# An adaLN-style block with attention and adapters: one x row tile's split, the rounding of the row maxima and the last steps' fillers are placed anew

## The chip, the cores and the metric

The kernel runs on one core of a Trainium2 chip. The metric is the device time in microseconds of one execution. A core has a matrix engine (TensorE, PE), three others (VectorE, DVE; ScalarE, ACT; GpSimd, POOL), a queue for transfers (SyncE, SP) and 16 DMA engines. Each engine works off its own instructions in the order in which they are written, and waits for the others through counting semaphores.

## The reference, cut to what matters

```python
def reference(x, ...):            # x: (8, 256, 1024) float32
    # 1. linear layer with a LoRA adapter per batch row, chosen by itok_B_0_23
    c = x @ W.T + b + 2.0 * (x @ A[itok]) @ Bm[itok]
    # 2. attention: 32 query heads, 8 key/value heads of 32, softmax over 256 keys
    q, k, v = c @ w_q, c @ w_k, c @ w_v
    weights = softmax(q @ k.T / sqrt(32));  x = x + (weights @ v) @ w_o
    # 3. per-row weight matrix (itok_B_3_7), then a routed low-rank FFN, top 2 of 4 experts
    z = x @ weight[itok2].T
    x = x + sum over experts of gate_e(z) * (z @ A_e.T) @ B_e.T * 4
```

## The kernel before

Matrices in float32 are split in a rounded high part (fp32r) and a low part, value minus high part, and multiplied as high x high + high x low + low x high. A split is thus two instructions: ScalarE rounds, and VectorE (for some tiles GpSimd) subtracts.

There are three stages. `fold_stage` multiplies W into the projection weights. `attend_stage` runs four pairs of batch rows (`PAIRS`), and in each pair 16 steps (`STEPS`), 64 steps in all; a step n is one key/value head of one batch row. `finish_stage` multiplies by w_o, adds to x, and does the routed FFN; its first pieces are woven into the last steps of attention through the functions `ahead_*`, and its `first()` and `second()` follow.

In a step TensorE's order is written out in `tensor.step`: scores 0 and 1 of head n (L926); the first part of the projection work that the table `WORK` gives this step (units such as q6, q7 for this pair and v0, v1 for the next; L854, L876 to L880); the outputs of head n-3 (L950) and their sums of exponentials (L954, from GpSimd's `p_sum`); the transpose of the maxima of head n-1 (L961); transposed scores 0 and 1 of head n-2 (L937); scores 2 and 3 of head n; the second part of the work; transposed scores 2 and 3. Projection units take turns in two PSUM banks (`bank`), and a unit starts when the one two before it has been read out (`free`).

VectorE's order in a step (`vector.step`): maxima 0 and 1 (L770), splits of x named in `X_LO[(s, 0)]` (L493), low parts of the units that the step before finished (`late(n - 1)`, L739), then maxima 2 and 3, then `split_maxima(n)`: a cast of the 128x8 negated maxima to fp32r (L776) and the subtraction for their low parts (L778), then `X_LO[(s, 1)]` and the reductions of value units (`soon(n, 1)`). In step 0 the low part of q1 is taken between maxima 1 and 2. Scores i of a head wait for maxima i-2 (`s_max`), the transpose waits for the low parts of the maxima (`nmax_lo`).

ScalarE's order (`scalar.step`): the copy of the transposed maxima (L699), exponentials 0 and 1 (L681), the output copy (L689), value copies (L667), `X_HI[(s, 0)]` (L489), exponentials 2 and 3, high parts of q and k units (`late(n)`, L646, four instructions of which the second signals a half), `X_HI[(s, 1)]`. GpSimd adds the exponentials (L630, `p_sum`) two steps after their scores, and takes the lower part of x tiles 2 and 4 (`X_LO_POOL`). SP queues the loads of x and of Wo, and the copies inside the chip.

```python
X_HI = {(10, 1): range(4), (11, 0): [4], (12, 0): [5, 6], (12, 1): [7]}
X_LO = {(11, 0): [0, 1], (11, 1): [3], (12, 1): [5, 6], (13, 0): [7]}
X_LO_POOL = {10: 2, 11: 4}
```

In the last steps (s = 12 and up of pair 3, and steps 64 to 66) `ahead_tensor` fills TensorE with w_o tiles (`one_tile`, L1239; tile 7 is done in two halves) and with rows of the first batch row's cond2 matrix (`cond_row`, L1284). A cond row is loaded by GpSimd (`load_cond`, L1187, into one of four buffers, after a register load of its index at L1183), rounded by ScalarE (L1265), and its low part is taken by VectorE (L1269). `residual` (L1230) adds a w_o tile to x; a tile waits for the residual two before it. `middle` (L1580) multiplies x by the turned product `g_t`. `first()` and `second()` are written out for each engine.

## Time and profile before

| | us |
|---|---|
| median of 3 runs | 1009.52 |
| lowest, highest | 1008.81, 1012.29 |
| the profiled execution | 1010.05 |
| its span | 1008.4 |
| TensorE busy | 987.5 (98%) |
| VectorE busy | 625.9 (62%) |
| ScalarE busy | 453.6 (45%) |
| GpSimd busy | 247.2 (25%) |

The span is the time from the first to the last instruction that the profiler recorded; 1.65 us of the execution lie around it. The granted TensorE clock was 0.998 over the span. A view of waits puts the idle time of an engine just before an instruction down to the one that released it. A line in the timeline gives start, length, engine, line, operation, what it writes and reads, the number of merged instructions, and in brackets the idle time before it with its releaser. Steps 0 to 63 run from 187.6 to about 692 us; pair changes (steps 9 to 14) lie at 250 to 298, 379 to 428 and 509 to 557 us and look alike; the first is shown.

### The profile page before, as it was taken

What the parts mean: (1) busy time and instruction counts of PE and PEld (TensorE: products, weight loads), DVE (VectorE), ACT (ScalarE), POOL (GpSimd) and SP (SyncE); (2) the same over time, 40 slices, a digit from 0 to 9 for tenths busy, and PEclk for the clock granted to TensorE, in tenths of its full rate; (3) what the DMA queues carried; (4) which work ended last, traced back from release to release, by engine and by line L of the source; (5) the groups of instructions that cost most, each with busy time, mean ns of one, the idle gap of its engine ahead of it and who ended that gap; (6) DMA issues with size and microseconds to landing.
All of it is one profiled execution on the core that took longest, in us unless ns stands there. A gap on an engine that the chain in (4) does not pass through costs nothing.

```text
span 1008.4 us, 16074 instructions
## 1 busy us (share of the span) xinstructions
PE 987.5 (98%) x6228; PEld 769.9 (76%) x6228; DVE 625.9 (62%) x1028; ACT 453.6 (45%) x806; POOL 247.2 (25%) x234
## 2 busy tenths in 40 slices
PE   9999999999999999999999999999999999999996
PEld 6878788777687776877777777786787778778775
DVE  6671822686946778467786688766664654654443
ACT  6121322365744657456665566747441432332221
POOL 1000001033422434223343247645110110110001
PEclk9999999999999999999999999999999999999999
DMA  7030411111411124111142424264999579463432
GB/s 274 0 105 1 136 48 56 43 44 39 128 36 44 50 59 123 44 44 49 44 114 79 110 74 138 86 170 185 276 298 251 165 248 243 143 223 108 164 125 84
DMA packets 72395, 117.33 MB, mean 116 GB/s; under 512 B 7698, under 2 KB 55186, under 8 KB 70816
## 3 DMA queue, kind: packets, MB, share of 16 engines
q1 hardware_dynamic: 62592, 81.70, 28.5%
q0 software_dynamic: 9728, 34.61, 10.0%
q8 instruction: 50, 0.82, 0.4%
q14 instruction: 25, 0.20, 0.1%
HBM read 86.38 MB, written 18.89 MB: 104 GB/s over the span
## 4 chain that ended last, share of the span: by engine, by line
PE 92%; DVE 4%; ACT 1%; POOL 1%; issue 1%; DMA 1%; POOLq 0%; ACTq 0%
PE psP L854 21%; PE psW L1239 17%; PE psF L292 12%; PE psG L1284 8%; PE psO L950 6%; PE psS L926 6%; PE psT L937 5%; PE psX L1580 3%; PE psO L954 3%; DVE nmax L770 2%; PE psF L303 2%; PE psP L876 2%; DVE q_stack L739 1%; PE psP L878 1%; PE psM L961 1%; PE psP L880 1%
## 5 line engine op out<-in xcount | busy, mean ns | idle before, releaser
L630 POOL TENSOR_TENSOR p_sum<-probs 128x512 f32<-128x512 f32 x128 | 168.5, 1317 | 331.7 <-ACT probs L681 331.7
L854 PE MATMUL psP<-x_hl,wq 128*128 128x512 f32 x960 | 237.2, 391 | 0.2 <-DVE v_sb L760 0.2
L770 DVE TENSOR_REDUCE nmax<-psS 128x2 f32<-128x512 f32 x256 | 164.5, 684 | 96.2 <-PE psS L926 91.8
L854 PEld LDWEIGHTS psP<-x_hl,wq 128*128 128x128 f32 x960 | 173.4, 188 | 31.2 <-DVE v_sb L760 0.4
L681 ACT ACTIVATE probs<-psT 128x512 f32<-128x512 f32 x256 | 139.0, 595 | 74.2 <-PE psT L937 73.4
L1239 PE MATMUL psW<-o_split,wq 128*128 128x512 f32 (+1 forms) x600 | 137.5, 383 | 0.0
L1239 PEld LDWEIGHTS psW<-o_split,wq 128*128 128x128 f32 x600 | 108.8, 188 | 21.4
L1269 DVE TENSOR_TENSOR cond_lo<-cond_raw,cond_hi 128x1024 fp32r<-128x1024 f32 x64 | 78.3, 1240 | 54.8 <-ACT cond_hi L1265 54.3
L1265 ACT ACTIVATE cond_hi<-cond_raw 128x1024 fp32r<-128x1024 f32 x64 | 66.5, 1057 | 82.9 <-PE psG L1284 70.2
L739 DVE TENSOR_TENSOR q_stack<-psP,q_stack 32x512 fp32r<-32x512 f32 x128 | 87.8, 686 | 10.2 <-ACT q_stack L646 8.3
L926 PEld LDWEIGHTS psS<-k_stack,q_stack 96*128 96x128 f32 x512 | 79.0, 189 | 16.5 <-DVE q_stack L739 2.1
L1187 POOL DMA_DIRECT2D cond_raw<-in_cond x64 | 33.9, 530 | 232.8 <-PE psG L1284 232.8
L937 PE MATMUL psT<-q_stack,k_stack 98*128 98x512 f32 x256 | 86.8, 418 | 0.0
L926 PE MATMUL psS<-k_stack,q_stack 96*128 96x256 f32 x512 | 84.6, 285 | 1.9 <-DVE nmax L770 1.3
L646 ACT ACTIVATE q_stack<-psP 32x512 fp32r<-32x512 f32 x128 | 75.1, 587 | 17.3 <-PE psP L861 15.8
L292 PE MATMUL psF<-q_hi,w_hi 128*128 128x512 f32 x184 | 71.8, 390 | 0.0
L292 PE MATMUL psF<-q_lo,w_hi 128*128 128x512 f32 x184 | 71.6, 389 | 0.0
L292 PE MATMUL psF<-q_hi,w_lo 128*128 128x512 f32 x184 | 71.6, 389 | 0.0
L950 PE MATMUL psO<-probs,v_sb 128*32 128x256 f32 x1024 | 68.5, 385 | 0.0
L699 ACT ACTIVATE nmax_rows<-psM 16x128 f32<-16x128 f32 x64 | 17.0, 266 | 105.1 <-PE psM L961 104.7
L950 PEld LDWEIGHTS psO<-probs,v_sb 128*32 128x32 f32 x1024 | 26.7, 109 | 30.1 <-issue 16.3
L1239 PE MATMUL psW<-wq 128*128 128x256 f32 x384 | 49.4, 283 | 0.0
(155 smaller groups left out, 1378.4 us busy)
## 6 DMA issues: line engine op xcount, KB each, us to landing
cond_raw<-in_cond POOLq DMA_DIRECT2D x64, 512.0 KB, 4.8
x_raw<-in_xT SPq DMA_DIRECT2D x32, 256.0 KB, 3.2
o_scratch<-o_sb SPq DMA_DIRECT2D x64, 128.0 KB
q_stack<-q_stack SPq DMA_DIRECT2D x31, 256.0 KB, 2.9
q_raw<-in_Wqkv SPq DMA_DIRECT2D x24, 256.0 KB, 3.9
o_pair<-rden_scratch SPq DMA_DIRECT2D x24, 256.0 KB, 9.0
o_pair<-o_scratch SPq DMA_DIRECT2D x6, 1024.0 KB, 13.9
w_raw<-in_W SPq DMA_DIRECT2D x8, 512.0 KB, 7.8
```

The source lines that it names most:

```text
L292: mm = pe.matmul(psF[:, bank(j, m)], w[:, k, m * P:(m + 1) * P], q[:, k], start=(k == 0 and i == 0), stop=(k == KT - 1 and i == 2))
L630: pool.tensor_tensor(p_sum[:, heads], probs[:, 0, heads], probs[:, 1, heads], ALU.add).then_inc(sum_done, 1)
L681: nc.scalar.activation(probs[:, i % 2, (i // 2) * 512:(i // 2 + 1) * 512], psT[:, i % 2], ACT.Exp, scale=ATT_SCALE).then_inc(exp_done, 1)
L739: ins = dve.tensor_tensor(to(h), both(psP[32 * h:32 * h + 32, bank(p, u)]), f(hi(h)), ALU.subtract)
L770: dve.tensor_reduce(nmax[:, n % 2, 2 * hp:2 * hp + 2, qt], psS[:, i % 2].rearrange("p (h k) -> p h k", h=2), AX.X, ALU.max, negate=True).t ...
L854: mm = pe.matmul(out, wq[:, i, w, k * P:(k + 1) * P], x[:, k, part], start=(k == 0 and n_ == 0), stop=False)
L926: mm = pe.matmul(psS[:, i % 2, j * T:(j + 1) * T], q_stack[0:96, slot, c, 2 * hp + j, qt * P:(qt + 1) * P], k_stack[0:96, c, g], start=Tru ...
L937: pe.matmul(psT[:, kt], k_stack[0:98, c, g, kt * P:(kt + 1) * P], q_stack[0:98, slot, c, 2 * hp:2 * hp + 2].rearrange("p h t -> p (h t)"), ...
L950: pe.matmul(psO[HD * h:HD * h + HD, 0], v_sb[p % 2][:, c, kt, g], probs[:, kt, h * T:(h + 1) * T], start=(kt == 0), stop=(kt == KK - 1))
L1239: mm = pe.matmul(out, wq[:, k, w, m * P:(m + 1) * P], o(part, k), start=(k == 0 and j == 0), stop=(k == KT - 1 and j == 2))
L1269: dve.tensor_tensor(cond_lo[r % RAW][:], cond_raw[r % RAW][:], f(cond_hi[:, r % SPLIT]), ALU.subtract).then_inc(cond_lo_done, 1)
L1284: mm = pe.matmul(psG[0:EC, half], a[:, k], w[:, half * 512:(half + 1) * 512], start=(k == 0 and i == 0), stop=(k == KT - 1 and i == 2))
```

## The change

The fourth row tile of x (tile 3) has its lower part taken in part 0 of step 11 and not in part 1; the rounding of tile 4 moves from part 0 to part 1. The maxima are rounded by ScalarE (a Copy activation, 128x8, SBUF to SBUF) behind exponentials 2 and 3 of the step, and VectorE takes their low parts one step on, behind maxima 0 and 1. In step 0 the low part of q1 moves behind maxima 3. In the last steps the first half of w_o tile 7 goes to step 64 ahead of cond row 0, its second half to step 65, and the halves that stood in `first()` and `second()` each move up by one place; their residuals move with them. The load of cond row 6 is issued by GpSimd between the two `p_sum` of the last head, and not behind them. ScalarE copies the turned product before it rounds cond row 9.

```diff
@@ -339,8 +339,8 @@
 
 
 X_LOAD = {(9, 0): [0, 1], (9, 1): [2], (10, 0): [3, 4], (10, 1): [5], (11, 0): [6, 7]}
-X_HI = {(10, 1): range(4), (11, 0): [4], (12, 0): [5, 6], (12, 1): [7]}
-X_LO = {(11, 0): [0, 1], (11, 1): [3], (12, 1): [5, 6], (13, 0): [7]}
+X_HI = {(10, 1): range(4), (11, 1): [4], (12, 0): [5, 6], (12, 1): [7]}
+X_LO = {(11, 0): [0, 1, 3], (12, 1): [5, 6], (13, 0): [7]}
 X_LO_POOL = {10: 2, 11: 4}
 SEQ = ["v0", "v1", "v2", "v3", "t", "k0", "q0", "q1", "q2", "r0", "r1", "q3", "k1", "q4", "q5", "q6", "q7"]
 NS = len(SEQ)
@@ -626,6 +626,8 @@
                 pool.wait_ge(exp_done, TILES * n + 2 * hp + 2)
                 if n and hp == 0:
                     pool.wait_ge(pv_done, n)
+                if n == N - 1 and hp == 1:
+                    ahead.gpsimd_last(pool)
                 heads = slice(hp * T2, (hp + 1) * T2)
                 pool.tensor_tensor(p_sum[:, heads], probs[:, 0, heads], probs[:, 1, heads], ALU.add).then_inc(sum_done, 1)
             if p + 1 < PAIRS and s + 2 in X_LO_POOL:
@@ -680,6 +682,11 @@
                 act.wait_ge(pv_done, n)
             nc.scalar.activation(probs[:, i % 2, (i // 2) * 512:(i // 2 + 1) * 512], psT[:, i % 2],
                                  ACT.Exp, scale=ATT_SCALE).then_inc(exp_done, 1)
+
+        def round_maxima(n):
+            act.wait_ge(s_max, TILES * (n + 1))
+            nc.scalar.activation(nmax_parts[:, n % 2, 0:8], nmax[:, n % 2].rearrange("p h q -> p (h q)"),
+                                 ACT.Copy).then_inc(nmax_hi, 1)
 
         def copy_o(n):
 
@@ -713,6 +720,8 @@
             if 2 <= n <= N + 1:
                 exp(n - 2, 2)
                 exp(n - 2, 3)
+            if n < N:
+                round_maxima(n)
             if more and s == 8:
                 split_a_hi(act, p + 1)
             for unit_ in late(n):
@@ -772,8 +781,6 @@
 
         def split_maxima(n):
             flat = nmax[:, n % 2].rearrange("p h q -> p (h q)")
-            dve.wait_ge(s_max, TILES * (n + 1))
-            dve.tensor_copy(nmax_parts[:, n % 2, 0:8], flat).then_inc(nmax_hi, 1)
             dve.wait_ge(nmax_hi, n + 1)
             dve.tensor_tensor(nmax_parts[:, n % 2, 8:16], flat, f(nmax_parts[:, n % 2, 0:8]),
                               ALU.subtract).then_inc(nmax_lo, 1)
@@ -784,10 +791,12 @@
             if n < N:
                 maxima(n, 0)
                 maxima(n, 1)
+            if 1 <= n <= N:
+                split_maxima(n - 1)
             if more:
                 for k in X_LO.get((s, 0), ()):
                     split_x_lo(dve, p + 1, k, x_lo_done)
-            for unit_ in late(n - 1) if n else [(0, "q1")]:
+            for unit_ in late(n - 1):
                 evacuate(*unit_)
             for unit_ in soon(n, 0):
                 if unit_[1] != "q0":
@@ -796,7 +805,8 @@
             if n < N:
                 maxima(n, 2)
                 maxima(n, 3)
-                split_maxima(n)
+            if n == 0:
+                evacuate(0, "q1")
             if p and n < N and s == 6:
                 invert(dve, p - 1)
             if more and s == 8:
@@ -1189,7 +1199,7 @@
 
     def gpsimd(pool):
         for n in range(B):
-            load_cond(pool, n, range(6, KT) if n == 0 else range(KT))
+            load_cond(pool, n, range(7, KT) if n == 0 else range(KT))
 
         pool.wait_ge(gated_done, B)
         for j in range(YT):
@@ -1315,6 +1325,8 @@
             dve.tensor_tensor(ra_lo[:], ra_raw[:], f(ra_hi[:]), ALU.subtract).then_inc(ra_lo_done, 1)
         if part == 1 and s == 14:
             normalise(dve, 1)
+        if part == 1 and s == 17:
+            residual(dve, KT - 1)
         for r in ROWS_LO.get((s, part), ()):
             cond_row_lo(dve, r)
         if part == 0 and s == 16:
@@ -1331,12 +1343,15 @@
         if s in ROWS_LOAD:
             load_cond(pool, 0, ROWS_LOAD[s])
 
+    def ahead_gpsimd_last(pool):
+        load_cond(pool, 0, [6])
+
     def ahead_tensor(pe, n, part):
         m = FIRST_TILES.get((n - LAST, part))
         if m is not None:
             one_tile(pe, 0, m)
-        if (n - LAST, part) == (17, 0):
-            one_tile(pe, 0, KT - 1, range(4))
+        if (n - LAST, part) in ((16, 0), (17, 0)):
+            one_tile(pe, 0, KT - 1, range(4) if n - LAST == 16 else range(4, KT))
         if (n - LAST, part) == (18, 1):
             pe.wait_ge(o_lo_done, 2)
             one_tile(pe, 1, 0, range(4))
@@ -1375,8 +1390,8 @@
             nc.scalar.activation(fb_stack[:], fb_raw[:], ACT.Copy).then_inc(fb_hi_done, 1)
             copy_g(0)
             cond_row_hi(act, KT)
+            turn_copies(0)
             cond_row_hi(act, KT + 1)
-            turn_copies(0)
 
         def second():
             gates(0)
@@ -1498,8 +1513,8 @@
         def first():
             cond_row_lo(dve, 6)
             dve.memset(beats[:], 0.0).then_inc(chain, 1)
+            residual(dve, KT)
             cond_row_lo(dve, 7)
-            residual(dve, KT - 1)
             before.invert(dve, PAIRS - 1)
             dve.wait_ge(fb_hi_done, 1)
             dve.tensor_tensor(fb_stack[ER:P], fb_raw[ER:P], f(fb_stack[ER:P]), ALU.subtract).then_inc(fb_lo_done, 1)
@@ -1507,10 +1522,10 @@
             cond_row_lo(dve, KT + 1)
 
         def second():
-            residual(dve, KT)
+            residual(dve, KT + 1)
             gates(0)
             for m in range(KT):
-                if m:
+                if m > 1:
                     residual(dve, KT + m)
                 if m < 6:
                     cond_row_lo(dve, KT + m + 2)
@@ -1613,18 +1628,19 @@
         def first():
 
             cond_row(pe, 5)
-            one_tile(pe, 0, KT - 1, range(4, KT))
+            one_tile(pe, 1, 0, range(4, KT))
             cond_row(pe, 6)
             cond_row(pe, 7)
-            one_tile(pe, 1, 0, range(4, KT))
+            one_tile(pe, 1, 1, range(4))
             turn_g(0)
-            one_tile(pe, 1, 1, range(4))
+            one_tile(pe, 1, 1, range(4, KT))
             middle(0)
 
         def second():
             cond_row(pe, KT)
             for m in range(1, KT - 1):
-                one_tile(pe, 1, m, range(4, KT) if m == 1 else range(KT))
+                if m > 1:
+                    one_tile(pe, 1, m)
                 cond_row(pe, KT + m)
             cond_row(pe, KT + 7)
             one_tile(pe, 1, KT - 1, range(4))
@@ -1681,7 +1697,7 @@
             y_two(B - 1, j, last_bank(j), y_done)
 
     ahead.sync, ahead.gpsimd, ahead.scalar, ahead.vector = ahead_sync, ahead_gpsimd, ahead_scalar, ahead_vector
-    ahead.tensor = ahead_tensor
+    ahead.tensor, ahead.gpsimd_last = ahead_tensor, ahead_gpsimd_last
     st.sync, st.gpsimd, st.scalar, st.vector, st.tensor = sync, gpsimd, scalar, vector, tensor
     return st
```

## Rows read from the trace of the kernel before

**Rows 1.** The profile's page: busy time of each engine, and the chain.

```profile
PE 987.5 (98%) x6228; PEld 769.9 (76%) x6228; DVE 625.9 (62%) x1028; ACT 453.6 (45%) x806; POOL 247.2 (25%) x234
...
PE 92%; DVE 4%; ACT 1%; POOL 1%; issue 1%; DMA 1%; POOLq 0%; ACTq 0%
```

**Rows 2.** Waits of TensorE: released by whom; us in total, times, longest.

```profile
PE psP L876 <- DVE q_stack L739: 2.6, 3, 0.9
PE psP L876 <- DVE x_hl L493: 1.8, 3, 0.6
...
PE psS L926 <- DVE nmax L770: 1.3, 2, 0.8
```

**Rows 3.** Timeline of TensorE, steps 12 to 14 of the first pair.

```profile
268.96 0.28 PE L880 MATMUL psP<-v_lo,x_hl 128*128 128x256 f32 x1
...
269.84 0.40 PE L876 MATMUL psP<-v_hi,x_hl 128*128 128x288 f32 x1 [0.60 <-DVE x_hl L493]
...
273.95 0.37 PE L876 MATMUL psP<-v_hi,x_hl 128*128 128x288 f32 x1 [0.86 <-DVE q_stack L739]
...
283.31 0.40 PE L876 MATMUL psP<-v_hi,x_hl 128*128 128x288 f32 x1
```

**Rows 4.** Groups by line: busy us, mean ns, idle before.

```profile
L776 DVE CAST nmax_parts<-nmax 128x8 fp32r<-128x8 f32 x64 | 38.8, 607 | 2.2
...
L778 DVE TENSOR_TENSOR nmax_parts<-nmax,nmax_parts 128x8 fp32r<-128x8 f32 x64 | 16.0, 250 | 2.2
...
L1354 ACT ACTIVATE gate<-shift 128x8 f32<-128x8 f32 x8 | 1.7, 208 | 26.6 <-DVE shift L1461 26.6
...
L511 ACT ACTIVATE v_hi<-a_raw 128x128 fp32r<-128x128 f32 x8 | 2.0, 308 | 0.0
```

**Rows 5.** Timeline of VectorE, steps 9 to 12, and step 15.

```profile
256.19 0.68 DVE L776 CAST nmax_parts<-nmax 128x8 fp32r<-128x8 f32 x1
...
256.99 1.28 DVE L770 TENSOR_REDUCE nmax<-psS 128x2 f32<-128x512 f32 x2
258.31 2.79 DVE L739 TENSOR_TENSOR q_stack<-psP,q_stack 32x512 fp32r<-32x512 f32 x4
261.12 1.29 DVE L770 TENSOR_REDUCE nmax<-psS 128x2 f32<-128x512 f32 x2
...
271.01 2.79 DVE L739 TENSOR_TENSOR q_stack<-psP,q_stack 32x512 fp32r<-32x512 f32 x4
...
308.82 1.22 DVE L778 TENSOR_TENSOR nmax_parts<-nmax,nmax_parts 128x8 fp32r<-128x8 f32 x1
```

**Rows 6.** Timeline of GpSimd, steps 10 and 15.

```profile
257.20 1.28 POOL L630 TENSOR_TENSOR p_sum<-probs 128x512 f32<-128x512 f32 x1 [0.36 <-ACT probs L681]
...
308.74 1.28 POOL L630 TENSOR_TENSOR p_sum<-probs 128x512 f32<-128x512 f32 x1 [7.71 <-ACT probs L681]
```

**Rows 7.** Timeline of ScalarE, end of step 9.

```profile
257.01 2.39 ACT L646 ACTIVATE q_stack<-psP 32x512 fp32r<-32x512 f32 x4
```

**Rows 8.** Timeline of TensorE, step 1.

```profile
192.99 1.01 PE L926 MATMUL psS<-k_stack,q_stack 96*128 96x256 f32 x4 [0.85 <-DVE nmax L770]
...
196.36 0.27 PE L961 MATMUL psM<-id_sb,nmax_parts 128*16 128x128 f32 x1
```

**Rows 9.** GpSimd: a register load, the DMA behind it, the last p_sum.

```profile
L608 POOLq TENSOR_LOAD <-idx_a x1: 283/283/283, 205.8 to 205.8; - x1
...
206.97 0.53 POOL L609 DMA_DIRECT2D a_raw<-in_lora_A  x1 [0.51 <-issue]
...
704.74 1.29 POOL L630 TENSOR_TENSOR p_sum<-probs 128x512 f32<-128x512 f32 x1 [0.57 <-ACT probs L681]
705.96 1.09 POOL L1187 DMA_DIRECT2D cond_raw<-in_cond  x2
```

**Rows 10.** Timeline of TensorE, step 64 and `first()`.

```profile
692.45 0.65 PE L1284 MATMUL psG<-cond_hi,ra_hi 128*68 128x512 f32 x2 [0.26 <-DVE nmax L770]
...
715.52 0.68 PE L1284 MATMUL psG<-cond_hi,ra_hi 128*68 128x512 f32 x2 [0.51 <-DVE cond_lo L1269]
```

**Rows 11.** Busy time by window: 713 to 750 us; clock, DMA share and GB/s last.

```profile
713.00:750.00 37.00, 35.93 (x251) 30.71 (x252) 24.44 (x40) 15.78 (x16) 4.23 (x8) 1.00 1.06 316
```

## Prediction

> **What bounds the kernel now.** I read the busy shares and the chain first: TensorE is busy 98% of the span and holds 92% of the chain that ended last, VectorE 4% [rows 1]. A gain has to come out of TensorE's gaps, so its waits are the next view: the three largest, on q low parts, on x's low parts and on maxima, sum to 5.7 us [rows 2]. These are idle times behind a modelled end; from start to start a gap is longer: the last product of one x tile starts at 268.96, the first of the next usually 0.12 us on, here at 269.84, so 0.76 us is lost where the view says 0.60 [rows 3]. Counted that way over TensorE's timeline, the gaps that the change can reach are: in steps 0 to 3 before maxima 1.2 and 0.9; in each of three pair changes 0.45 (maxima), 0.76 (x's fourth row tile), 1.03 (the bank of q7) and 0.30 (value copies); and between 692 and 721 0.54, 0.37, 0.89, 0.68 and 0.41. That is 2.1 + 7.6 + 2.9 = 12.6 us. The question is which of them only change their name.
>
> **VectorE's relief.** The cast goes: 64 of 607 ns, 38.8 us of VectorE; the subtraction stays (250 ns mean) [rows 4]. But a cast such as that of 256.19 ends at 256.87, 0.03 after the p_sum that ran beside it on GpSimd: most of its time is a wait. The moved subtraction stands after the next step's first two maxima. In step 10 these started at 256.99; with the cast and the subtraction gone from before them they can start at 256.51 (0.44 after their scores) and end at 257.79, in the middle of the p_sum of 257.20 to 258.48 [rows 5, 6]. Does a subtraction wait for it too? Its usual row is 0.17 us; but at 308.82, begun 0.08 after a p_sum, it took 1.22 and ended with it [rows 5, 6]. I take "it waits": it ends at 258.50 and the q evacuation starts at 258.54, where it was 258.31.
>
> The Trainium skill (SBUF — State Buffer, "SBUF: two separate sides") has the rule behind this: a VectorE instruction with two SBUF inputs and a GpSimd one that reads SBUF exclude each other for the whole instruction; the row at 308.82 agrees. By the 0.17 us of the usual row the subtraction would end at 257.99, by the rule at 258.50.
>
> Even without that hold little is won, for ScalarE arrives at the same time: its new rounding stands before its q copies. I price it at 0.2 us by the 128x8 exponential, 208 ns; bounds 0.15 (part of it overlaps its neighbour) and 0.31 (the copies of 128x128) [rows 4]. Copies that began at 257.01 begin at 257.2 and are half done at 258.4 instead of 258.2 [rows 7]. So evacuations that open the second half of a step move back by 0.2 to 0.3 us.
>
> **Where that costs.** The maxima of 261.12 become 261.35 [rows 5], and TensorE, which already waits for them at 261.96, goes on 0.24 later; that is inside the pair sum below. Elsewhere: 0.1 each in step 3 of pairs 1 and 2, 0.2 in step 3 of pair 3, 0.25 in step 11 of pair 3, where scores stand within 0.2 us of their maxima: +0.65. The other steps have over 0.8 us between maxima and scores; no cost there.
>
> **The split of x, three times.** The fourth tile's lower part moves ahead of the second-half maxima and ends near 267.3; TensorE's 0.76 goes [rows 3], so the products behind it come 0.57 earlier, the 0.24 counted. ScalarE, relieved of the fifth tile's rounding here, begins its last two exponentials at 268.44; their p_sum runs from 269.6 to 270.89; the subtraction is held until 270.92, and the evacuation of q7 starts at 270.95 instead of 271.01 [rows 5]. Its end frees the bank that TensorE waits for at 273.95 [rows 3]. So the 0.76 is given back to that wait but for 0.06. The fifth tile (rounded from 272.0 to 272.6, lower part on GpSimd until 273.9) is wanted at 276.4: hidden, with 2.5 us to spare; what queues behind its rounding on ScalarE, a row copy and two exponentials, comes 0.4 later under as much cover. Two steps on, the value block's reductions no longer stand behind cast and subtraction, 0.8 us, ScalarE's copy comes as much earlier, and the 0.30 before 283.31 goes [rows 3]. Per pair -0.36, in all -1.1.
>
> **Steps 0 to 3.** q1's evacuation now follows the second maxima. The scores of 192.99 lose their wait, 1.2 us with the pair behind them [rows 8]. But the evacuation (2.79 from 191.88) ends at 194.67, the maxima of step 1 at 195.98, the subtraction at 196.18, and the transpose, which TensorE now reaches at 195.1, cannot start before 196.3: it stood at 196.36 [rows 8]. ScalarE's rounding waits in step 1 for maxima that end at 198.2 and holds q2's copies behind it, 1.6 us; q2 is read in step 4, so that is hidden. Step 3 starts at 204.07 instead of 204.21: -0.14.
>
> **The last steps (from 692).** Half of tile 7 now stands before the first cond row: 12 products, 1.43 us. It fills the 0.54 before 692.45 [rows 10] and 0.27 of the 0.37 before 700.61, and from there on one more half tile is done by each point. Against that, GpSimd's load of cond row 6 now stands between the wait for the last exponentials and the last p_sum, with SP's queue untouched. Exposed are a register load and the issue: such a pair takes from 205.8 to 206.97 until the DMA starts and 0.53 for itself, 1.7 us; the lower bound is the 0.51 of idle printed there plus 0.53, 1.04. The p_sum of 704.74 is that much later, and the last sums (at 706.08, with under 0.1 us of slack) move to about 708.4 with the shift of the half tile [rows 9]. The load itself, issued at 705.96 before, is issued at about 706.5: not earlier. Row 7's load behind it moves from 706.51 to 708.4 and lands near 713.1 to 714; TensorE wants the row at 716.3 and it is ready at 716.8, after rounding, a residual and 1.23 of subtraction. Sum: gone 0.54 + 0.27 + 0.89 + 0.68 + 0.41 = -2.8 (the last three are the waits for cond rows, such as that before 715.52, and for the g copies [rows 10]); new 1.7 and 0.5. SP starts its big loads when the last output is copied, 2.3 us later, into a stretch in which the DMA engines are full (share 1.06 [rows 11]); one of them landed 0.6 us before VectorE used it, and the residual behind is waited for: 0.3 to 0.8, I take 0.4. Together -0.2; bounds -1.3 and +2.0.
>
> **Sum.** +0.65 - 1.1 - 0.14 - 0.2 = -0.8 us. Against the profiled execution's 1010.05 (1008.4 of span and 1.65 around it) that is 1009.25; the median of the runs is 0.53 below it, so 1008.7.
>
> **Rivals.**
> (a) The gaps close for good: 2.1 in steps 0 to 3, 3 x 1.06 for tile and value copies, 2.9 at the end, nothing given back: -8.2, 1001.3. For it: 38.8 us off the engine that ends most of TensorE's waits [rows 2, 4]. Against: two independent releases (the held subtraction, ScalarE's half) stand at the same 258.5, and the transpose of step 1 hangs on the moved subtraction. Half of it, -4 (1005.5), is the least that I would call faster; it takes an undelayed p_sum (-1.7) and a q7 evacuation that starts right behind its maxima (3 x 0.5).
> (b) Slower by one mechanism: the register load before the last p_sum shifts the chain of the last output and with it the o and x loads on full DMA engines. If TensorE waits for them in the second stage (725 to 750) by the full 2.3 us instead of 0.4, the whole is +1.1; if their landing stretches twice as far, +4, 1013.5. It decides once the residual before tile 14 is over 3 us late.
> (c) ScalarE's rounding waits for late maxima and blocks its queue: q copies, then exponentials. At 0.2 us in half of 64 steps, +6, 1015. Against it: before most of its row copies ScalarE is idle for 1 us or more.
> (d) The waits move and little else happens: my forecast.
>
> **Chances and range.** Within 0.3% (3.0 us, about what a measurement tells from no change), which is (d) with the mild ends of (a) and (b): 0.67. (a) from its half on 0.21; (b) and (c) beyond 3 us 0.12. So faster 0.21, same 0.67, slower 0.12. The likeliest case alone has 1007.0 to 1011.3: the last steps' bounds, and the rounding at 0.15 or 0.31 in ten places. With the cases of both signs, 1005.0 to 1011.6.
>
> **What the profile after would show.** Right: subtractions of 0.6 to 0.7 us where p_sum runs beside them; TensorE's wait for the tile gone, the one for q7 still about 1 us; the one for value copies gone; the last p_sum over 1 us after the last exponential, a register load between. Wrong: subtractions of 0.17 in all steps; a q7 wait under 0.5; cond row 6 landing before 710; the chain running through DMA between 735 and 750; or exponentials that follow the rounding late in most steps.

## Result and profile after

The change made the kernel slower: 1015.64 us median (1009.80 to 1018.40, 17 runs) against 1009.51 (1008.21 to 1012.41, 17 runs), ratio 1.0047 with a 95% interval of 1.0035 to 1.0059. Forecast was 1008.7, within 1005.0 to 1011.6. The profiled execution took 1016.2 us with a span of 1014.5, 6.1 more than before. The runs of the changed kernel scatter: 4 of 17 lie under 1011, the others between 1012.0 and 1018.4. The trace is of one of the latter; none exists of the four.

The page of the changed kernel, busy shares and chain, where [rows 1] stand for before. SP's queue is new in the chain, and DMA has 3% where it had 1%:

```profile
PE 987.4 (97%) x6228; PEld 769.9 (76%) x6228; DVE 609.8 (60%) x964; ACT 461.5 (45%) x870; POOL 246.0 (24%) x234
...
PE 89%; DVE 5%; DMA 3%; SPq 1%; issue 1%; POOL 1%; ACT 1%; POOLq 0%; ACTq 0%
```

TensorE's waits after (by whom it was released; total, times, longest). Against [rows 2] the wait for x's low parts is gone, the one for q's grew, and two are new: the residual (`x_even`, L1240, L1230 before) and the last p_sum:

```profile
PE psW L1249 <- DVE x_even L1240: 6.0, 2, 5.0
PE psP L886 <- DVE q_stack L748: 3.4, 3, 1.1
PE psO L964 <- POOL p_sum L632: 2.0, 1, 2.0
```

**The attention steps** gained as meant. TensorE's timeline after, which answers to [rows 3]: the x tile's products follow each other 0.12 us apart, and the wait for q7's bank is longer (1.31 us from start to start, 1.03 before):

```profile
268.22 0.28 PE L890 MATMUL psP<-v_lo,x_hl 128*128 128x256 f32 x1
268.34 0.29 PE L886 MATMUL psP<-v_hi,x_hl 128*128 128x288 f32 x1
...
272.87 0.37 PE L886 MATMUL psP<-v_hi,x_hl 128*128 128x288 f32 x1 [1.14 <-DVE q_stack L748]
```

Measured from step 0 (187.58 before, 187.09 after: that half microsecond arose in the fold, ahead of every edited line, and is noise: step 0 starts between 186.7 and 187.6 in all seventeen traces) step 4 starts 0.51 earlier, step 16 1.01, step 62 1.49. These distances repeat well: from step 0 to step 62 the five traces with the attention of before take 488.26 to 488.38 us, the ten with that of after 486.72 to 486.85.

**From step 62 to the end** 8.1 us were lost: 332.6 us before, 340.6 after. All of it lies ahead of `middle(1)`, the second product of x with a turned g: from its start to the end all traces of all kernels take 253.4 us. GpSimd and TensorE around the last p_sum, after ([rows 9] before):

```profile
704.94 0.55 POOL L1197 DMA_DIRECT2D cond_raw<-in_cond  x1 [2.11 <-issue]
705.52 1.27 POOL L632 TENSOR_TENSOR p_sum<-probs 128x512 f32<-128x512 f32 x1
```
```profile
706.84 0.64 PE L964 MATMUL psO<-p_sum,ones 128*32 128x256 f32 x8 [2.03 <-POOL p_sum L632]
```

That is 2.2 us. Still, `middle(0)` starts 0.8 us earlier than before, with half a tile more done. From step 62 to that point TensorE takes 46.1 us where it took 44.9, of which 1.43 are the additional products: so far nothing is lost. From `middle(0)` to `middle(1)` it takes 41.2 us instead of 34.3. SP stores the last outputs 0.8 us later than before (708.17, before 707.41), but begins load_o(2) 1.2 us earlier (712.64, before 713.84). SP's queue, then VectorE, then TensorE, in the second stage:

```profile
719.31 4.02 SPq L475 DMA_DIRECT2D rden_scratch<-rden_sb  x1
723.37 3.44 SPq L1119 DMA_DIRECT2D o_pair<-rden_scratch  x4
726.86 0.85 SPq L1121 DMA_DIRECT2D o_pair<-o_scratch  x1
```
```profile
747.46 2.29 DVE L1212 TENSOR_TENSOR o_pair<-o_pair 128x2048 f32<-128x2048 f32 x1 [5.80 <-DMA o_pair<-o_scratch]
749.66 0.42 DVE L1240 TENSOR_TENSOR x_even<-x_even,psW 128x256 f32<-128x256 f32 x1
```
```profile
740.58 3.12 PE L1249 MATMUL psW<-wq 128*128 128x256 f32 x24 [0.95 <-DVE x_even L1240]
...
750.14 4.62 PE L1249 MATMUL psW<-wq 128*128 128x256 f32 x24 [5.04 <-DVE x_even L1240]
```

Read it backwards: TensorE waits for a residual; the residual stands in VectorE's queue behind the normalisation of o(3); that one waits for load_o(3)'s last transfer, issued at 726.86 and landed 20.6 us later (before: issued 724.27, landed 741.0, used at 741.59). And 24 products behind the wait take 4.62 us where the same 24 took 3.12 ten microseconds earlier. The windows 740 to 760, before and then after (busy us of TensorE, its weight loads, VectorE, ScalarE and GpSimd; granted clock, DMA share and GB/s last), show why: the granted clock was at the upper of its two levels (2.4 GHz) before, and 0.91 of that in the mean after, behind a pause of 5 us.

```profile
740.00:760.00 20.00, 19.82 (x143) 17.31 (x142) 15.46 (x24) 9.42 (x10) 2.12 (x4) 1.00 0.86 265
```
```profile
740.00:760.00 20.00, 14.38 (x92) 12.45 (x93) 11.62 (x11) 8.26 (x7) 2.11 (x4) 0.91 0.70 233
```

### The profile page after: what moved, and what is told of

Read it like the earlier page. It is cut to its first block, busy times and chain, and to the rows that moved or that the text cites. A ratio compares the mean times of both kernels' runs of the same rounds, so it can differ in the third digit from the quotient of the medians.

```text
span 1014.5 us, 16077 instructions
## 1 busy us (share of the span) xinstructions
PE 987.4 (97%) x6228; PEld 769.9 (76%) x6228; DVE 609.8 (60%) x964; ACT 461.5 (45%) x870; POOL 246.0 (24%) x234
## 3 DMA queue, kind: packets, MB, share of 16 engines
q0 software_dynamic: 9728, 34.61, 10.5%
## 4 chain that ended last, share of the span: by engine, by line
PE 89%; DVE 5%; DMA 3%; SPq 1%; issue 1%; POOL 1%; ACT 1%; POOLq 0%; ACTq 0%
PE psP L864 20%; PE psW L1249 16%; PE psF L292 12%; PE psG L1294 7%; PE psS L936 6%; PE psO L960 6%; PE psT L947 6%; PE psO L964 3%; PE psX L1595 2%; DVE q_stack L748 2%; DMA o_pair<-o_scratch 2%; PE psP L886 2%; PE psF L303 2%; PE psP L888 2%; DVE nmax L779 1%; PE psP L890 1%
## 5 line engine op out<-in xcount | busy, mean ns | idle before, releaser
L936 PEld LDWEIGHTS psS<-k_stack,q_stack 96*128 96x128 f32 x512 | 79.2, 189 | 15.9 <-issue 2.4
L1249 PEld LDWEIGHTS psW<-wq 128*128 128x128 f32 x384 | 49.3, 196 | 8.3 <-DVE x_even L1240 6.9
```

The lines of the kernel that those rows point to most:

```text
L936: mm = pe.matmul(psS[:, i % 2, j * T:(j + 1) * T], q_stack[0:96, slot, c, 2 * hp + j, qt * P:(qt + 1) * P], k_stack[0:96, c, g], start=Tru ...
L1249: mm = pe.matmul(out, wq[:, k, w, m * P:(m + 1) * P], o(part, k), start=(k == 0 and j == 0), stop=(k == KT - 1 and j == 2))
```

## Experiments

All ratios are to the kernel before on the same chip, with 95% intervals; a ratio can differ a little from the quotient of the two medians, since the runs scatter unevenly. Where two variants were measured on different chips, their ratios say more than their medians.

### The change in parts

Theory T says: row 6's load delays the last p_sum, with it SP's loads, and o(3) lands late. Its rivals put the loss on the 2 us by which everything comes earlier (A) or on the new order of tiles, rows and residuals (F).

**e1_no_row6** is the change without this part:

```diff
-                if n == N - 1 and hp == 1:
-                    ahead.gpsimd_last(pool)
...
-            load_cond(pool, n, range(7, KT) if n == 0 else range(KT))
+            load_cond(pool, n, range(6, KT) if n == 0 else range(KT))
```

> The whole change, but cond row 6 is loaded after the last p_sum, as before. Theory T (the load before the last p_sum delays the p_sum, the last output copy and with it SP's big loads; load_o(3) then lands 6 us late and TensorE waits 5 us for the residual in front of tile 14): the o loads land as before, the wait of 5 us is gone, and the attention part's gain stays: 1006 to 1008, ratio 0.996 to 0.999. Rival A (the attention part's shift by 2 us is what collides with the DMA traffic) and rival F (the order of row loads, residuals and tiles at the end does it): the wait of 5 us stays, 1012 to 1015. Rival R: row 6 lands too late for its new place, a new wait of 1 to 2 us before cond row 6, 1008 to 1010.

**e2_row6_only** is the converse: the kernel before with only that load moved.

> The kernel before with cond row 6's load moved ahead of the last p_sum and nothing else. Theory T: p_sum 1.7 to 2.2 us later, the last output copy as much, the loads behind it land 3 us or more later and the normalisation of o(3) holds the residual behind it: +4 to +7 us, 1014 to 1017, ratio 1.004 to 1.007. Rivals A and F: only the p_sum wait itself, less what later waits give back, +1 to +2 us, ratio 1.001 to 1.002.

**e3_attn_only** has the x split, the rounding on ScalarE and the new place of q1's evacuation (the copy out of PSUM with its low part), and the last steps of before; **e4_tail_only** the last steps' part and the attention of before.

> The x split, the maxima's rounding on ScalarE and q1's evacuation moved; the last steps are those of before. By my sum of the prediction -0.6 us; by the step starts of the changed kernel's trace -1.8 to -2.0 us: 1007.5 to 1009, ratio 0.998 to 0.9995. Rival A: everything 2 us earlier is what makes the big loads collide: a wait of some us for a residual between 740 and 752, 1011 to 1014.

> The last steps' part alone: half tiles, row and residual order, row 6's load ahead of the last p_sum; the attention steps are those of before. Theory T or rival F: the wait of 5 us in front of tile 14 is there, 1014 to 1018, ratio 1.004 to 1.008 (the changed kernel without the gain of 1.5 to 2 us in the attention part). Rival A: no such wait, 1009 to 1011.

Measured: e1 1008.91 us, ratio 0.9992 (0.9981 to 1.0003); e2 1018.22, 1.0082 (1.0068 to 1.0095); e3 1008.55, 0.9986 (0.9970 to 1.0002); e4 1015.63, 1.0063 (1.0043 to 1.0083). Rival A falls with e3, rival F with e1: the one load of 512 KB, placed one instruction further ahead, costs 6.7 us with the rest of the change and 8.8 without it (by the ratios 5.5 and 8.3). Rival R has no large part: e1 waits 0.25 us for one row's low part. But e1 isn't as fast as T had it, and e2 is slower. TensorE in e1, second stage, has two waits where before had none:

```profile
737.31 3.13 PE L1247 MATMUL psW<-wq 128*128 128x256 f32 x24 [0.46 <-DVE x_even L1238]
...
742.76 3.14 PE L1247 MATMUL psW<-wq 128*128 128x256 f32 x24 [0.92 <-DVE x_even L1238]
```

From start to start they are 0.62 and 1.09 us. From step 62 to `middle(0)` the fillers save e1 2.3 us (43.99 us with 1.43 of additional products, before 44.87), and between there and `middle(1)` 1.8 come back (34.61 us with 1.43 less to do, before 34.27): TensorE meets the o loads that much earlier. What is left over is too little for single traces: to the end e1 takes 332.0 us, e3 332.3 and the kernel before 332.5, but two more kernels with the same last steps as before 331.5 (e8 below) and 333.5 (e7 below). By the ratios e1 is no faster than e3.

e2 lost its time elsewhere. ScalarE, then TensorE, in e2:

```profile
723.30 1.06 ACT L1267 ACTIVATE cond_hi<-cond_raw 128x1024 fp32r<-128x1024 f32 x1 [3.01 <-DMA cond_raw<-in_cond]
724.26 0.67 ACT L1372 ACTIVATE g_t<-psX 128x272 f32<-128x272 f32 x2
```
```profile
708.09 2.80 PE L1241 MATMUL psW<-wq 128*128 128x256 f32 x12
...
724.98 6.79 PE L1585 MATMUL psX<-g_t,x_even 128*128 128x68 f32 x32 [3.29 <-ACT g_t L1372]
731.52 1.10 PE L1286 MATMUL psG<-cond_hi,ra_hi 128*68 128x512 f32 x2
...
736.20 0.63 PE L1286 MATMUL psG<-cond_hi,ra_hi 128*68 128x512 f32 x2
```

ScalarE's copies of g stood behind the rounding of row 9, whose load was late. TensorE paused 3.3 us, and then two products of 128x512 took 1.10 us instead of 0.63: it ran at the lower level, 1.2 GHz, until about 735 (0.50 in the windows 728 to 731 and 731 to 734). `middle(0)` took 6.79 us; in e1 the same 32 products take 3.69. Behind the pause of 2.1 us for the p_sum, too, the clock fell here (0.57 from 708 to 710, 0.58 to 712): 12 products took 2.80 us, where 1.60 is usual. So e2's loss in its trace is two pauses, 5.5 us from start to start, and the clock behind each, 1.2 and 3.1 us in these two groups alone, less some waits of before that are gone. The change's order (copies of g ahead of row 9's rounding) takes just this trap away, and steps into the next.

### The p_sum's delay, or the load's place?

**e13_reg_only** delays the last p_sum in the kernel before by one register load and moves no DMA:

```diff
+                if n == N - 1 and hp == 1:
+                    pool.value_load(idx_sb[0:1, 0:1], min_val=0, max_val=7)
```

> The kernel before, with one more register load ahead of the last p_sum, whose value nothing uses, and no DMA moved. Theory T: the p_sum is 0.5 to 1.2 us late, the last output copy and SP's loads as much: +1 to +4 us, 1010.5 to 1013.5; that prices the register load alone. Rival D (only the moved DMA matters): within 0.5 us of the kernel before. Rival C (a TensorE pause of this length costs more by its clock): a stretch below 0.95 of the clock between 705 and 760.

**e10_row6_early** puts row 6's load one p_sum further ahead, at `hp == 0`, before the wait for the exponentials.

> The whole change, but row 6's load stands one p_sum further ahead, before the wait for the exponentials of the last step's first half, where GpSimd idles 1.3 us. Theory T (what costs is the delay of the last p_sum by register load and issue, with all that hangs on it): the wait of 2.2 us before the last sums goes, load_o(3) lands before 742: 1006.5 to 1009, ratio 0.997 to 0.9995. Rival D (the earlier row load itself crowds the DMA engines and delays SP's loads): no wait before the sums, but load_o(3) still lands after 745, 1012 to 1015.

**e19_rows67_ahead** puts the loads of rows 6 and 7 both there, `load_cond(pool, 0, [6, 7])` at `hp == 1`.

> The whole change, but the loads of rows 6 and 7 both stand ahead of the last p_sum, back to back as they were before. Rival D2 (splitting the two loads is what slows the engines between 709 and 724): rates there back to 320 and 290 GB/s, load_o(3) lands by 743, 1010 to 1012 in spite of a p_sum 0.6 us later still. Theory Q: the p_sum and load_o(3) come out later still, 1015.5 to 1019.

e13: 1010.49, 1.0012 (0.9993 to 1.0032). The register load made the p_sum 0.56 us later (idle 1.13 instead of 0.57 before it), TensorE waited 0.67 for it, and nothing else moved: load_o(3) landed at 740.8. T's first half is right, and at this size cheap. e10: 1015.43, 1.0039 (1.0018 to 1.0059), though TensorE's pause for the p_sum fell from 2.2 to 1.1 us: load_o(3) landed at 747.0, though SP had begun load_o(2) at 710.3, 3.5 us earlier than before (1.2 counted from step 62). So T falls: neither the delay of the p_sum nor a late start of SP's loads is what costs. e19: 1011.38, 1.0018 (1.0004 to 1.0033), with the longest wait for the p_sum of all (2.42 us from start to start). VectorE and TensorE in e19:

```profile
742.77 2.29 DVE L1213 TENSOR_TENSOR o_pair<-o_pair 128x2048 f32<-128x2048 f32 x1 [2.08 <-DMA o_pair<-o_scratch]
```
```profile
707.05 0.64 PE L964 MATMUL psO<-p_sum,ones 128*32 128x256 f32 x8 [2.24 <-POOL p_sum L632]
...
745.45 3.14 PE L1250 MATMUL psW<-wq 128*128 128x256 f32 x24 [1.31 <-DVE x_even L1241]
```

With both loads ahead the change is 3 to 4 us faster than with row 6's alone (2.9 by the ratios, 4.3 by the medians), although the p_sum comes later still. The profiled execution of e19 is its fastest of ten. Why it helps isn't shown: D2 had asked for 320 and 290 GB/s between 709 and 724, and there were 253. And in e2, where the two loads are also apart, load_o(3) landed early (738.0): being apart isn't enough to delay it.

### What o(3) waits for on its way

Theory O: with row 6 ahead, load_o(2) gets onto the engines before row 9's load and both suffer. **e14_o2_behind_row9** holds load_o(2) back in the changed kernel, **e16_row9_late** holds row 9's load back in the kernel before, by three register loads.

```diff
         before.load_den(sp, PAIRS - 1)
+        sp.wait_ge(cond_used, 7)
         load_o(sp, 2)
```

> The whole change, but SP waits, between the load of the denominators and load_o(2), until cond row 6 has been used, 2.3 us behind the issue of row 9's load. Theory O (the runs with row 6's load ahead are slow where load_o(2) gets onto the DMA engines before row 9's load does, because the earlier row 6 lets the denominators return sooner; then row 9 lands 9 instead of 6 us after its issue, o(2) after 18 instead of 13 us, and load_o(3) near 747): load_o(2) begins 2.4 us later and still lands earlier, near 729 to 731; row 9 lands near 719; load_o(3) lands by 743; the wait of 5.2 us before tile 14 is under 2 us: 1009 to 1011.5, ratio 1.000 to 1.002. Rival T (what counts is how late SP's loads start): load_o(2) later by 2.4 us makes it worse, 1016 to 1020. Rival D2 (the order of rows 6 and 7 alone slows the engines): no difference from the changed kernel, 1015 to 1016.

> The kernel before, with row 9's load alone held back by three register loads on GpSimd, some 1.5 to 2 us, so that it comes amid load_o(2)'s first transfers; TensorE's own use of row 9 has 5 us to spare. Theory O: row 9 takes 8 us or more to land, load_o(2) lands after 732, load_o(3) after 744, TensorE waits 2 to 5 us for a residual between 740 and 752: 1012 to 1016, ratio 1.003 to 1.006. Rivals T and D2 (row 9's place does not matter by itself): within 0.7 us of the kernel before.

e14: 1016.29, 1.0065 (1.0044 to 1.0086). Row 9 landed at 718.0 (after: 721.7), as O had it, but load_o(2) at 731.7 and load_o(3) at 747.2: O falls for the changed kernel. e16: 1016.58, 1.0055 (1.0033 to 1.0077), but not by O's way: row 9 landed at 722.3, and the trap of e2 closed (a pause of 4.5 us before `middle(0)`, and half speed from 723 until 732). O asked for a late load_o(3); it landed at 741.0.

Theory Q: SP issues load_o(3) too late, behind row 12's load. **e17_o3_first** is the changed kernel with load_o(3) ahead of the store of the last reciprocals, which it doesn't need.

```diff
-        before.store_rden(sp, PAIRS - 1)
         load_o(sp, 3)
+        before.store_rden(sp, PAIRS - 1)
```

> The whole change, but SP loads o(3) before it waits for the last reciprocals and stores them, not after (o(3) needs only reciprocals stored long before). Theory Q (with row 6's load ahead, load_o(3) gets out of SP's queue behind the load of row 12 instead of 2 us ahead of it, as in every kernel with the 5 us wait; then rows 12 to 14 share the engines with it): the o(3) loads are issued 1 to 4 us earlier, ahead of row 12's, and land by 743; the wait before tile 14 is under 2 us: 1009 to 1011.5, ratio 1.000 to 1.002. Rival K (SP issues only as the engines free its earlier loads, whatever the order): o(3)'s last load is still issued at 726 and lands at 746 to 748, 1014 to 1016.

e17: 1013.72, 1.0030 (1.0011 to 1.0048), with runs at 1010 and at 1016. In the profiled one SP began load_o(3) at 715.6 instead of 723.4, and still issued its last transfer at the same time as before:

```profile
715.59 11.28 SPq L1119 DMA_DIRECT2D o_pair<-rden_scratch  x4
726.90 1.42 SPq L1121 DMA_DIRECT2D o_pair<-o_scratch  x1
```

So rival K is right for this stretch: an SP instruction that is reached earlier just stands longer. The table sets the kernels side by side, all from traces, one of each: GB/s from 709 to 724, when load_o(2)'s fourth transfer of reciprocals landed, when SP issued load_o(3)'s last transfer, when GpSimd issued row 12's load, when load_o(3) landed, and TensorE's wait before tile 14 (start to start). The execution traced isn't always typical of its kernel: for instance those of e1, e4 and e19 took 1.3 to 1.9 us less than the median, that of e17 3.1 more.

| kernel | GB/s | o(2) fourth | o(3) issued | row 12 issued | o(3) landed | wait |
|---|---|---|---|---|---|---|
| before | 301 | 724.5 | 724.3 | 726.5 | 741.0 | 0 |
| e1 | 308 | 722.3 | 721.9 | 723.4 | 740.1 | 1.1 |
| e3 | 299 | 722.6 | 722.4 | 724.1 | 739.3 | 0 |
| e7 | 255 | 725.7 | 725.1 | 725.3 | 741.0 | 0 |
| e8 | 305 | 722.7 | 723.4 | 725.4 | 740.3 | 0 |
| e9 | 307 | 722.2 | 723.4 | 723.9 | 740.6 | 0 |
| e13 | 304 | 724.4 | 724.1 | 725.9 | 740.8 | 0 |
| e18 | 314 | 720.8 | 721.9 | 723.6 | 740.2 | 0 |
| e19 | 253 | 723.0 | 724.3 | 725.9 | 742.7 | 1.5 |
| e2 | 263 | 723.4 | 724.7 | 735.0 | 738.0 | 0 |
| e16 | 279 | 725.6 | 726.8 | 733.9 | 741.0 | 0 |
| e4 | 249 | 727.7 | 727.0 | 727.1 | 745.0 | 2.7 |
| after | 266 | 727.5 | 726.9 | 725.7 | 747.4 | 5.2 |
| e5 | 254 | 727.0 | 726.1 | 725.5 | 747.6 | 0 |
| e10 | 241 | 726.7 | 726.4 | 724.6 | 747.0 | 6.7 |
| e14 | 256 | 726.9 | 726.0 | 725.2 | 747.2 | 6.5 |
| e17 | 246 | 727.8 | 726.9 | 726.5 | 747.3 | 4.9 |

In every trace load_o(3)'s last transfer goes out within 1.3 us of the landing of load_o(2)'s fourth one. Where it lands at 745 or later, these two stand at 726 to 728, otherwise at 721 to 726, but for e16's issue at 726.8. The rate between 709 and 724 doesn't tell: e7 and e19 have 255 and 253 GB/s and an early landing. How long the transfer takes goes with row 12's load: 20.4 to 21.6 us in the five kernels in which that went out first, 15.9 to 18.4 in the ten in which it went out up to 2.3 us behind, and 13.3 and 14.2 in e2 and e16, where a pause of TensorE had held it back to 735.0 and 733.9. So a later issue is paid for twice, once by itself and once because GpSimd's row loads are then on the engines first; no run moved the row loads alone to prove it. The Trainium skill (DMA: Bandwidth & Descriptors, "Queues, rings and completion order") says that an engine takes turns between its queues packet by packet; the longer landing beside GpSimd's row loads agrees with it. Why load_o(2) is 3 us later with row 6's load ahead, and not when row 7's goes with it (e19) nor in e2, no run here settles.

### The cover on VectorE

Cover is here the work that TensorE can still do before something late holds it up.

**e5_norm_late** is the whole change with o(3) normalised two tiles later; **e9_no_row6_norm_late** is e1 with the same edit; **e18_e9_o3_first** adds e17's edit to e9.

```diff
-                if m in (2, 3):
-                    normalise(dve, m)
+                if m in (2, 5):
+                    normalise(dve, 2 if m == 2 else 3)
```

> The whole change, but VectorE normalises o(3) two tiles later (behind the residual and the lower part of m = 5), so that a late load_o(3) holds no residual in front of tiles 12 to 14. If the wait of 5.2 us in front of tile 14 is the landing of load_o(3) held in VectorE's queue: the wait and the stretch at 0.91 of the clock behind it go, 1008 to 1010.5, ratio 0.999 to 1.001, while load_o(3) still lands near 747. Rival L (the loads of x, not o(3), hold the residuals, or TensorE meets the next late load as soon as it gets there): another wait of 2 us or more between 740 and 760, 1012 to 1015.

> Row 6 loaded after the last p_sum, as before, and o(3) normalised two tiles later; the rest of the change stands. The waits of 0.62 and 1.09 us for residuals at 737 and 743 that the kernel without the row load has: the second goes, the first (behind o(2)'s normalisation) stays: 1 us less than that kernel, 1007.5 to 1008.5, ratio 0.998 to 0.999. Rival: DMA landings set this stretch whatever VectorE's order, no difference from the kernel without the row load, 1008.9.

> The best kernel so far (row 6 behind the last p_sum, o(3) normalised two tiles later) with load_o(3) ahead of the store of the reciprocals. Theory Q: o(3) lands 1 to 3 us earlier, but nothing waits for it there any more; the wait of 0.6 us before middle(1) or the residual's stays: within 0.5 us of that kernel, 1006.5 to 1007.5, ratio 0.996 to 0.998. Rival K: the reciprocals' store and x_odd's loads are later, a new wait further on: 1008 or more.

e5: 1011.23, 1.0015 (1.0002 to 1.0027), a little more than expected and 4.4 us less than the change by the medians and 3.2 by the ratios. load_o(3) lands as late as before the edit, but no residual that TensorE soon needs stands behind its normalisation any more. VectorE and TensorE in e5:

```profile
747.64 2.29 DVE L1212 TENSOR_TENSOR o_pair<-o_pair 128x2048 f32<-128x2048 f32 x1 [1.10 <-DMA o_pair<-o_scratch]
```
```profile
752.84 0.71 PE L1584 MATMUL psY<-id_sb,g_sb 68*128 68x68 f32 x8 [1.63 <-ACT g_sb L1377]
```

The 5 us became 1.8 (start to start) at the next customer, g's copy, which stands behind the rounding of o(3) in ScalarE's queue. e9: **1007.00 us (1006.66 to 1007.57, 9 runs), ratio 0.9966 (0.9954 to 0.9978)**, faster than both kernels and with the least scatter of all. Of e1's two waits the second is gone, as expected; 0.45 us of idle time before g's turn are new. The 2.6 us that the ratios put between e1 and e9 don't show in the traces, which take 1007.34 and 1007.57: the one of e1 is its fastest run, the one of e9 its slowest. So the edit took away the slower runs, and what they waited for wasn't seen. e18: 1007.27, 0.9967 (0.9957 to 0.9977), the same. SP issued load_o(3) at 721.9 instead of 723.4, and it landed at 740.2 instead of 740.6: little earlier, and nothing waits for it there.

### The attention part by its edits

**e7_x_only** has only the split of x moved, **e8_round_only** only the rounding on ScalarE.

> The kernel before with only the split of x's fourth and fifth row tiles moved. Of each pair change: the wait before the fourth row tile of x (0.76 us) goes, the one for the bank of q7 (1.03) grows by 0.4 to 0.7; by the step starts of the trace -0.1 to -0.4 us per pair, -0.2 to -1.2 in all. If the freed time is not given back, -2.2 in all.

> The kernel before with only the rounding of the maxima on ScalarE and VectorE's subtraction a step on (q1's evacuation as before). By my sum: the value copies' waits go (3 x -0.30), the later evacuations cost +0.65: -0.2 to -0.3 us by step 62. If the evacuations are later by ScalarE's 0.2 us in half of the 64 steps: +6. If the waits before the x tile and for q7 fall with the relief of VectorE: -1.5 or less.

One run each, read by step starts. From step 0 to step 62: 488.26 us before, 486.77 after, 486.72 in e3, 486.54 in e7, 488.13 in e8. The split alone brings 1.72, more than all the attention edits together and more than the 0.2 to 1.2 that I had expected of it; the relief of VectorE by 38.8 us of casts brings 0.13 (0.2 to 0.3 expected), hardly more than traces of one and the same attention differ (0.12 and 0.13). Neither has the 0.51 of steps 0 to 3, which q1's new place brings. From step 4 on the split alone gains 1.7 us, split and rounding together 1.0: on top of the split the rounding costs 0.8. The change without the rounding wasn't tried. In e7 TensorE's wait for q7's bank is as before, not longer:

```profile
272.91 0.38 PE L876 MATMUL psP<-v_hi,x_hl 128*128 128x288 f32 x1 [0.87 <-DVE q_stack L739]
```

The tile's subtraction (0.68 us) had stood ahead of q7's evacuation in VectorE's queue; taken out, it let maxima and evacuation (269.98, where it was 271.01 [rows 5]) come 1.03 earlier, of which 0.44 is by how much earlier e7 reaches step 11.

## Why the prediction was wrong

**The attention part** was right in what waits for what, and came out at -1.49 us where the sum had -0.59. Its steps, one by one:

- "It waits" (the subtraction for the p_sum that runs beside it): right. Its group after has a mean of 657 ns with 795 as the median, where its usual row was 170; VectorE's casts are gone and the waits in them moved to the subtractions: 38.8 + 16.0 us before [rows 4], 42.1 after. ScalarE's rounding at 0.2 us: right, 211 ns.

```profile
L785 DVE TENSOR_TENSOR nmax_parts<-nmax,nmax_parts 128x8 fp32r<-128x8 f32 x64 | 42.1, 657 | 0.0
```
```profile
L688 ACT ACTIVATE nmax_parts<-nmax 128x8 fp32r<-128x8 f32 x64 | 13.5, 211 | 3.1 <-DVE nmax L779 3.0
```

- The maxima before step 11: TensorE waits 0.49 us from start to start instead of 0.26, forecast 0.24 more. Right.
- The x tile's 0.76 "is given back to that wait but for 0.06": right. The wait for the tile and the one for the value copies are gone, the one for q7 has grown. Step 11 starts 1.01 us ahead of where the forecast had it (262.20), and as much ahead run the p_sum that holds the subtraction (forecast 269.6) and q7's evacuation (270.95, measured 269.94). From step 11 to q7's product it is 11.99 us before and 11.68 after: -0.31, forecast -0.30, with the 0.24 counted apart. To step 16 it is -0.73, forecast -0.60. In e7 the way from step 11 to q7's product is shorter by 0.60: without the moved subtraction nothing is held, and nothing given back.

```profile
268.61 1.28 POOL L632 TENSOR_TENSOR p_sum<-probs 128x512 f32<-128x512 f32 x1 [0.41 <-ACT probs L683]
```

- Steps 0 to 3: -0.51 by the start of step 4, forecast -0.14. The transpose waits for the moved subtraction, as forecast. A wait of 0.36 us that TensorE had at 197.30 went too; the sum had left it out.

```profile
195.63 0.28 PE L971 MATMUL psM<-id_sb,nmax_parts 128*16 128x128 f32 x1 [0.83 <-DVE nmax_parts L785]
```

- Of the costs of +0.65 in later pairs 0.45 were put into pair 3, with no gain of the split left to set against them there; from step 48 to step 62 TensorE takes 0.07 us more than before. What took the rest of them away was not followed up.

**The last steps** are where it failed, and not in their first half. Up to `middle(0)` the working had the gaps right (-2.8), the price of register load and issue nearly (1.7 forecast, 2.2 measured), and the wait for row 7 (0.5 forecast, 0.4 measured, 0.25 of it in the view of waits): together -0.2, and 46.1 - 1.43 - 44.9 is -0.2. The failing step is the term "I take 0.4" for SP's big loads on full DMA engines: measured are 5.2 and 1.1 us of waits for residuals, 0.3 for a row's low part at 738, and 1.5 us of clock in the 24 products behind the long wait (4.62 against 3.12). Its premise failed too, that SP starts its big loads 2.3 us later: load_o(2) began 1.2 us earlier than before, or 0.8 later if counted from step 62, and load_o(3)'s last transfer landed 6.5 us later (8.4 from step 62). Rival (b) named place and point of decision (the residual before tile 14, over 3 us late) and a time of 1013.5. What it had wrong is its cause: a delay of the p_sum by 0.56 us leaves the landing where it was (e13), a load placed so that it delays the p_sum less is as slow (e10), and one that delays it more is faster (e19). The place of row 6's load counts, together with that of row 7's; how, is open. The price of the later landing was bounded by the 2.3 us of the shift; a landing isn't shifted, it is re-dealt: SP's issue of one store stood still for 4.02 us where it had taken 0.34. Two of the signs of being wrong that the prediction named came true: the chain runs through DMA between 735 and 750 (a piece of it, start and length, stands below), and row 6 landed before 710 (708.7), since its load was issued at 704.9 and not at about 706.5; most of that is that everything runs 2 us earlier.

```profile
726.86 20.58 DMA o_pair<-o_scratch
```

It should have warned that before, o(3) landed 0.6 us ahead of its use, with TensorE's residual queued directly behind that use: a cover of 0.6 us on engines with a share of 1.06 [rows 11] is none.

The fillers' -2.8 was also counted as kept. In e1 they save 2.3 us up to `middle(0)`, and 1.8 come back behind it: the gaps around 700 turn into residual waits at 737 and 743. That is the case "the waits move and little else happens", at another place than looked for. With the normalisation moved as well (e9) the ratio falls from 0.9992 to 0.9966.

**Open**: why load_o(2) gets its reciprocals 3 us later in the changed kernel. It scatters between 1010 and 1018 us with one and the same program, so little decides it; that this is the order of transfers is a guess, for none of its four runs under 1011 was traced. Holding back rows 12 to 14 instead was not tried.

## What to carry to other kernels

When DMA engines are full for 30 us, don't price a moved load by its own shift: look which consumer has the least slack behind those engines, and what stands in that consumer's queue. First move that consumer away from the critical instruction (one line here, worth 2 to 3 us on the good version and 3 to 4 on the bad one), then fill gaps. And test each edit of a bundle by itself: here x's split carried most of the gain, row 6's load all of the loss, and 38.8 us taken off an engine were worth 0.13, or a loss on top of the split.

## What the hardware showed

- SP's DMA instructions can stand in its queue while its earlier transfers are under way: the store of 64 KB of reciprocals took 0.34 us to issue before, 4.02 after; one of the x loads 7.71; load_o(3), begun 7.8 us earlier, had its last transfer issued at the same time (e17).
- In the last steps of these traces every pause of TensorE of over 2.5 us (2.5 in e4 to 6.5 in e10) cost a second time by its clock. After 3.3 us of idle time (e2) it ran at the lower level for about 10 us, after 5.0 (the changed kernel) for about 3.5 (0.53 in 750 to 752, 0.61 in 752 to 754). After the 1.9 to 2.2 us of idle time before the last sums it fell for 3.4 us in e2 and not at all in the six kernels with the change's last steps, the changed one among them. These have closed two short waits ahead of it, of 0.54 and 0.36 us, that e2 has; that this is the reason is not shown.
- A register load on GpSimd in front of a p_sum costs 0.56 us (e13); with the issue of a DMA that uses it, TensorE's wait for the p_sum is 2.1 us (e2) and 2.2 us (the changed kernel); with two such issues 2.4 (e19).
- The 128x8 subtraction on VectorE takes 0.17 us alone and 0.78 beside a p_sum on GpSimd, with which it ends (269.91 and 269.89 in the changed kernel).
